# Scores, exponentials and value products reordered by two query tiles, and the 16-bit product rows copied on GpSimd from the second batch on

## The chip, the cores and the metric

One NeuronCore of a Trainium2 chip. The metric is the device time of the whole program in microseconds (us). In this document PE is TensorE (matmuls), PEld its weight loads, DVE is VectorE, ACT is ScalarE, POOL is GpSimd and SP is SyncE, whose queue issues the DMAs.

## What is computed

Two recurrent layers over an input of 4 batches, 512 tokens and 512 features. Each layer is a normalisation, an attention branch, a feed-forward branch, and `x = x + attention * silu(feed-forward)`. The change touches the first layer only, whose reference is, cut to what matters:

```python
xn = layernorm(x)
q = (xn @ Wq)   # 32 heads of 16
k = (xn @ Wk)   # 8 key heads of 16, each used by 4 query heads
v = (xn @ Wv)   # 8 value heads of 16
attn = softmax(einsum('bhqd,bhkd->bhqk', q, k) / 4).astype(float16)
s = einsum('bhqk,bhkd->bhqd', attn, v) @ Wo
y = fwht(xn * SU_ug) / 64
y = silu(y @ W_gate.T * scale_g) * (y @ W_up.T * scale_u)     # 2048 wide
g = silu((fwht(y * SU_dp) / 64) @ W_down.T * scale_d)
x = x + s * g
```

The second layer (a delta-rule recurrence and a sign feed-forward) follows and is the same in both kernels.

## The kernel before, in words

`layer0` writes one program for each engine, and all of them run over the same counter `t` of **steps**. The attention is cut into 32 **units** (4 batches x 8 key heads, `NKV`). A unit has 4 **query tiles** of 128 queries, and a query tile takes two steps, so a unit has `STEPS` = 8 steps, a batch `BSTEPS` = 64, and there are 256 steps with scores. `m` is the step within its batch. What happens to one query tile, for its group of 4 query heads:

- PE, even `t`: `scores(t // 2)` (L1106) makes 4 matmuls, one for each head, into 4 PSUM banks (`vpair` and `bank`). It waits until all 4 exponentials of the tile before are made, since there are only these 4 banks.
- DVE: `row_max` (L623), 4 reductions of 128x512, each for one bank.
- ACT: `exps` (L922), 4 exponentials of 128x512 into `probs` (3 buffers, `TAKEN`); two of them at step `t` and two at `t + 1`.
- SP, two steps later: `turn_probs` (L339) issues a DMA transpose of the whole tile from `probs` to its columns of `probsT`.
- PE, at `t % 8 == PV_STEP` = 2 of the unit after: `weigh(u)` (L1117) makes the 16 value products of the unit from all 4 turned tiles at once. It waits for the DMA transposes of all of them. It stands right behind the scores of that step.
- DVE: `to_tokens`, `divide`, `to_features` (L659 to L689) at steps 3, 4 and 6 of the next unit; POOL takes over the division (L450) from unit 5.

Beside the attention, PE works at the feed-forward branch, whose results go through two PSUM banks, `GB`. In steps `m >= FFN_STEP` = 32 of a batch (the **gate half**) each step is one chunk of 8 matmuls (`ffn_mm`, L1143): at even steps the gate of 128 rows, at odd steps the up projection. ACT makes the tanh of the gate (`tanh_gate`, L941) and DVE multiplies it (`gate_mul`, L633), which frees the gate's bank; DVE then forms the product rows in 32 bit (`up_mul`, L646, into `row32`, a part of `th`), which frees the up bank; ACT copies them to 16 bit (`high_rows`, L898) and POOL subtracts to get the low half (`low_rows`, L443). `up_mul` of the next rows waits for that subtraction, because `row32` is one buffer. In steps `m < 32` of the batch after (the **down half**) each step is 6 matmuls with these rows (`down_mm`, L1157 to L1159) and, four times, an output projection (`project_o`, L1102) and the residual. During the first batch the weights are prepared as well: steps 0 to 31 transform the up and gate weights (`transform_ug`, L1055, `high_half`, `low_half`, and `chunk_pairs` on POOL), steps 16 to 68 the down weights (`dn_pair` on POOL, L412, `transform_dn`, `high_down`, `low_down`).

The order on each engine is the order of the program text in the loop over `t`, written out by hand. Waits are semaphores, and a waiting instruction holds up all behind it on its engine. At an even step of the gate half PE has

```python
if t < NU * STEPS and t % 2 == 0:
    scores(t // 2)
if t % STEPS == PV_STEP and 0 <= t // STEPS - 1 < NU:
    weigh(t // STEPS - 1)
```

and behind it the 8 matmuls of the step. The keys and queries of a unit reach their 4 slots by `load_heads` (L300): 8 small DMAs in a row, issued by SP at `t % 8 == 6`, between the DMA transposes.

Of the kernel before, what the change touches and what calls it, by code (L numbers as in the profile page):

```python
# [11 lines left out]
P = 128  # L12
# [22 lines left out]
PV_STEP, TOKEN_STEP, DIVIDE_STEP, TURN_BACK = 2, 3, 4, 6  # L35
# [120 lines left out]
def layer0(nc, d, x1_dram, W):  # L156

    ctx = ExitStack()
    with ctx:  # L159
# [113 lines left out]
        def _(sp):  # L273
# [26 lines left out]
            def load_heads(u):  # L300
# [28 lines left out]
            def load_raw(i):  # L329
                if i == 0:  # L330
                    sp.wait_ge(S["pv_done"], NU)
# [7 lines left out]
            def turn_probs(n):  # L339
# [7 lines left out]
            load_heads(0)  # L347
            load_heads(1)
            sp.dma_start(wsd[:, :], d["wscale_dp"].partition_broadcast(P)).then_inc(S["wo_in"], 16)
            for t in range(TEND):  # L350
# [14 lines left out]
                if t % STEPS == STEPS - 2 and 1 < t // STEPS + 2 < NU:  # L365
                    load_heads(t // STEPS + 2)
# [15 lines left out]
        def _(pool):  # L382
# [55 lines left out]

            def low_rows(b, ft):
# [24 lines left out]
            for t in range(TEND):  # L464
# [28 lines left out]
                if fb < B and fm >= FFN_STEP and t % 2 == 0 and (fb or (fm - FFN_STEP) // 2 >= LOW_FIRST):  # L493
                    low_rows(fb, (fm - FFN_STEP) // 2)
# [6 lines left out]
        def _(v):  # L501
# [158 lines left out]
            def to_tokens(u):  # L660

                v.wait_ge(S["pv_done"], u + 1)
# [116 lines left out]
            for t in range(TEND):  # L779
# [35 lines left out]
                if t % STEPS == TURN_BACK and 0 <= t // STEPS - 1 < NU and t // STEPS % 2 == 0:  # L815
                    to_features(t // STEPS - 1)
# [22 lines left out]
        def _(a):  # L839
# [74 lines left out]
            def evict_v(b):  # L914

                a.wait_ge(S["mb_full"], MB["v", b] + 1)
                if b >= 2:
                    a.wait_ge(S["pv_done"], (b - 1) * NKV)
# [58 lines left out]
            for t in range(TEND):  # L977
# [12 lines left out]
                if 0 <= t - PREP - 2 < NCH * KT:  # L990
                    high_half(t - PREP - 2)
# [5 lines left out]
                if t % 16 == Q_STEP + 1 and t // 16 + 1 < NU // 2:  # L997
                    evict_q(t // 16 + 1)
                if m == V_STEP + 1 and b + 1 < B:
                    evict_v(b + 1)  # L1000
                if m == K_STEP + 1 and b + 1 < B:
                    evict_k(b + 1)
                if t > FFN_STEP + 1 and (t - 2) // BSTEPS < B and (t - 2) % BSTEPS >= FFN_STEP and t % 2 == 0:
# [1597 lines left out]
```

## Time and profile before

| | us |
|---|---|
| three timed runs, median (lowest to highest) | 1487.92 (1484.96 to 1489.20) |
| the profiled execution | 1479.72 |
| its span, first to last instruction | 1477.9 |
| busy in the span: PE, DVE, ACT, POOL | 1278.4, 1058.7, 775.1, 524.5 |
| first layer with scores, 21.4 to 782.5 | 761.1 |
| rest of the first layer, to about 850 | 67 |
| second layer, from about 850 | 628 |

The mean granted TensorE clock is 0.963 of full speed over the span. The times of this table are one execution and three others; the profiled one is 8.2 us below the median. In the stretch with scores PE, DVE and ACT work in lockstep on one query tile at a time, so the busy shares there say little by themselves: the start of each tile's scores is the beat, and what delays it is what costs.

### The profile page before, as it was taken

What the parts mean: (1) busy time and instruction counts of PE and PEld (TensorE: products, weight loads), DVE (VectorE), ACT (ScalarE), POOL (GpSimd) and SP (SyncE); (2) the same over time, 40 slices, a digit from 0 to 9 for tenths busy, and PEclk for the clock granted to TensorE, in tenths of its full rate; (3) what the DMA queues carried; (4) which work ended last, traced back from release to release, by engine and by line L of the source; (5) the groups of instructions that cost most, each with busy time, mean ns of one, the idle gap of its engine ahead of it and who ended that gap; (6) DMA issues with size and microseconds to landing.
All of it is one profiled execution on the core that took longest, in us unless ns stands there. A gap on an engine that the chain in (4) does not pass through costs nothing. (4 is left out here: it accounts for less than half of the span.)

```text
span 1477.9 us, 22423 instructions
## 1 busy us (share of the span) xinstructions
PE 1278.4 (87%) x8226; PEld 640.0 (43%) x8226; DVE 1058.7 (72%) x1823; ACT 775.1 (52%) x1308; POOL 524.5 (35%) x434
## 2 busy tenths in 40 slices
PE   4777788777877787877888899999999999999998
PEld 2232333232322233322333355585548654765466
DVE  6688877666766567656777498687878688669846
ACT  5676666554655557545661775236533554246532
POOL 2389853002210022100221156323733274317531
PEclk9899999998999999999999999999999999999999
DMA  7775545565555665565657502300230111210221
GB/s 242 187 168 99 92 91 90 105 123 104 92 104 98 130 114 98 106 119 114 112 102 227 212 20 55 86 16 29 55 71 23 37 45 43 55 37 19 55 48 44
DMA packets 346557, 135.52 MB, mean 92 GB/s; under 512 B 312176, under 2 KB 333392, under 8 KB 343888
## 3 DMA queue, kind: packets, MB, share of 16 engines
q1 hardware_dynamic: 334032, 132.52, 40.6%
q10 hardware_dynamic: 12416, 1.57, 1.0%
q8 instruction: 66, 1.08, 0.3%
q14 instruction: 43, 0.35, 0.1%
HBM read 44.87 MB, written 17.87 MB: 42 GB/s over the span
## 5 line engine op out<-in xcount | busy, mean ns | idle before, releaser
L929 ACT ACTIVATE probs<-vpair,top_n 128x512 f16<-128x512 f32 x256 | 164.4, 687 | 256.3 <-DVE top_n L627 256.3
L1143 PE MATMUL bank<-rows,both 128*128 128x512 f16 x1024 | 244.7, 392 | 5.2 <-DVE fd L700 4.1
L627 DVE TENSOR_REDUCE top_n<-vpair 128x1 f32<-128x512 f32 x256 | 164.5, 684 | 84.9 <-PE bank L1114 82.8
L443 POOL TENSOR_TENSOR h<-th,h 128x512 f16<-128x512 f32 x61 | 71.5, 1172 | 271.5 <-ACT h L898 271.5
L627 DVE TENSOR_REDUCE top_n<-bank 128x1 f32<-128x512 f32 x256 | 163.7, 681 | 0.0
L929 ACT ACTIVATE probs<-bank,top_n 128x512 f16<-128x512 f32 x256 | 162.6, 690 | 0.0
L1143 PEld LDWEIGHTS bank<-rows,both 128*128 128x128 f16 x1024 | 97.5, 100 | 144.5 <-issue 35.4
L2218 PE MATMUL bank<-rows,both 128*128 128x512 f16 x512 | 118.3, 382 | 0.0
L1114 PE MATMUL vpair<-qk 32*128 32x512 f16 x256 | 50.4, 389 | 74.4 <-ACT probs L929 74.4
L2234 PE MATMUL bank<-both,hid 128*128 128x512 f16 x512 | 111.2, 379 | 0.0
L1128 PE MATMUL bank<-probsT,vaug 128*32 128x512 f16 x512 | 45.3, 487 | 72.3 <-DMA probsT<-probs 60.4
L1157 PE MATMUL bank<-dn,h 128*128 128x512 f16 x256 | 104.1, 407 | 0.9 <-DVE tg L633 0.9
L2202 PE MATMUL bank<-rows,both 128*128 128x512 f16 (+1 forms) x456 | 104.0, 379 | 0.9 <-PEq L159 0.9
L1158 PE MATMUL bank<-dn,h 128*128 128x512 f16 x256 | 103.1, 403 | 0.0
L1159 PE MATMUL bank<-dn,h 128*128 128x512 f16 x256 | 102.4, 400 | 0.0
L633 DVE SCALAR_TENSOR_TENSOR tg<-tg,bank 128x512 f32<-128x512 f32 x64 | 44.0, 687 | 72.3 <-ACT tg L941 71.8
L456 POOL TENSOR_TENSOR otok<-oblk,rl 128x256 f16<-128x256 f32 x25 | 15.5, 620 | 180.0 <-DVE rl L673 180.0
L2234 PEld LDWEIGHTS bank<-both,hid 128*128 128x128 f16 x512 | 50.1, 98 | 60.4
L2218 PEld LDWEIGHTS bank<-rows,both 128*128 128x128 f16 x512 | 48.4, 100 | 55.4 <-issue 0.8
L1114 PEld LDWEIGHTS vpair<-qk 32*128 32x128 f16 x256 | 12.9, 91 | 131.3 <-ACT probs L929 74.2
L2202 PEld LDWEIGHTS bank<-rows,both 128*128 128x128 f16 (+1 forms) x456 | 43.6, 98 | 55.5 <-issue 4.4
L1593 POOL TENSOR_TENSOR big<-big,both 128x384 f32<-128x384 f32 x32 | 32.0, 1026 | 94.5 <-DMA big<-t_scratch 70.3
(362 smaller groups left out, 2673.3 us busy)
## 6 DMA issues: line engine op xcount, KB each, us to landing
h<-in_ug SPq DMA_DIRECT2D x8, 1024.0 KB, 5.8
lt_scratch<-big SPq DMA_DIRECT2D x16, 384.0 KB, 2.7
dn<-in_down SPq DMA_DIRECT2D x2, 2048.0 KB, 11.1
x_scratch<-th SPq DMA_DIRECT2D x16, 256.0 KB, 2.6
res<-x_scratch SPq DMA_DIRECT2D x16, 256.0 KB, 4.1
out_x<-res SPq DMA_DIRECT2D x16, 256.0 KB, 2.0
both<-in_w SPq DMA_DIRECT2D x2, 1548.0 KB, 11.9
t_scratch<-tok SPq DMA_DIRECT2D x16, 192.0 KB, 2.1
```

The source lines that it names most:

```text
L443: pool.tensor_tensor(h16(ft, 1), row32, h16(ft, 0), ALU.subtract).then_inc(S["row_lo"], 1)
L627: v.tensor_reduce(top_n[:, i:i + 1], SC_[n % G][:, :], AX.X, ALU.max, negate=True).then_inc(S["max_done"], 1)
L929: a.activation(probs[:, k % TAKEN, j * T:(j + 1) * T], SC_[j][:, :], ACT.Exp, bias=top_n[:, i:i + 1]).then_inc(S["p_ready"], 1)
L1114: pe.matmul(SC_[j][:, :], qs[32 * j:32 * j + 32, u % SLOTS, qt * P:(qt + 1) * P], ks[32 * j:32 * j + 32, u % SLOTS, :], start=True, stop=T ...
L1128: mm = pe.matmul(OB[32 * j:32 * j + 32, :], vaug[:, b % 2, kt, g, :], probsT[:, TT * j + kt, :], start=kt == 0, stop=kt == TT - 1)
L1143: mm = pe.matmul(GB[n % 2][:, :], w[:, kt, col:col + P], xnb(b, kt), start=r == 0, stop=r == 2 * KT - 1)
L1157: pe.matmul(bk, h16(ft, 0)[:, rows], dn16(ft, 0), start=j == 0, stop=False)
L1158: pe.matmul(bk, h16(ft, 0)[:, rows], dn16(ft, 1), start=False, stop=False)
L1159: mm = pe.matmul(bk, h16(ft, 1)[:, rows], dn16(ft, 0), start=False, stop=j == FT - 1)
L2202: mm = pe.matmul(bk, lhs(i, kt), rhs(j, kt), start=n == 0, stop=n == 3 * KT - 1)
L2218: mm = pe.matmul(fbank[ht % 2][:, :], up[:, kt, ht * P:(ht + 1) * P], x_half(i, kt), start=kt == 0 and i == 0, stop=kt == KT - 1 and i == 1)
L2234: mm = pe.matmul(fbank[tt % 2][:, :], hid[:, i, ht, tt * P:(tt + 1) * P], down[:, ht, :], start=ht == 0 and i == 0, stop=ht == HT - 1 and ...
```

## The change

1. The unit's value products are cut in two: `weigh(n)` now takes 2 query tiles (256 columns) and is called at `t % 4 == 0` for the pair whose scores began 8 and 6 steps earlier. Before, the last tile's scores began 4 steps earlier. `to_tokens`, `divide` and `to_features` move by 1, 2 and 4 steps.
2. `load_heads` is split: `load_k` at `t % 8 == 6`, `load_q` at `t % 8 == 2`.
3. Of the feed-forward matmuls of an even step, 4 or 3 (gate half, `GATE_AHEAD`) or 1 or 0 (down half, `DOWN_AHEAD`) now stand ahead of the scores; so do the turns of x and the weight transforms of the first batch.
4. On ACT, `high_half` (first batch) stands ahead of the exponentials; `high_rows` of the first batch moves to the front of the step; from the second batch on it is an instruction of POOL. Evictions of q, k and v come one step later from step 70 on, behind the second pair of exponentials.

```diff
-PV_STEP, TOKEN_STEP, DIVIDE_STEP, TURN_BACK = 2, 3, 4, 6
+TOKEN_STEP, DIVIDE_STEP, TURN_BACK = 4, 6, 2
+GATE_AHEAD, DOWN_AHEAD = (4, 3), (1, 0)
+LATE_EVICT = 70
...
-            def load_heads(u):
+            def load_k(u):
...
                 for j in range(G):
                     sp.dma_start(ks[32 * j:32 * j + DH, slot, :], kst[DH * g:DH * g + DH, :]).then_inc(S[f"heads_in{slot}"], 16)
+
+            def load_q(u):
+
+                slot = u % SLOTS
                 sp.wait_ge(S["mb_took"], MB["q", u // 2] + 1)
+                if u >= SLOTS:
+                    sp.wait_ge(S["s_ps"], (u - SLOTS + 1) * SC)
                 for j in range(G):
...
                 if u:
-                    sp.wait_ge(S["pv_done"], u)
+                    sp.wait_ge(S["pv_done"], n // 2 - 1)
                 sp.dma_start_transpose(probsT[:, :, qt * P:(qt + 1) * P], probs[:, n % TAKEN, :]).then_inc(S[f"pt_in{n % TAKEN}"], 16)
...
-                if t % STEPS == STEPS - 2 and 1 < t // STEPS + 2 < NU:
-                    load_heads(t // STEPS + 2)
+                if t % STEPS == 6 and t // STEPS + 2 < NU:
+                    load_k(t // STEPS + 2)
+                if t % STEPS == 2 and 1 < t // STEPS + 1 < NU:
+                    load_q(t // STEPS + 1)
...
+            def high_rows(b, ft):
+                pool.wait_ge(S["gb_took"], GO["gu", b, 2 * ft + 1] + 1)
+                pool.tensor_copy(h16(ft, 0), row32).then_inc(S["row_hi"], 1)
...
                 if fb < B and fm >= FFN_STEP and t % 2 == 0 and (fb or (fm - FFN_STEP) // 2 >= LOW_FIRST):
+                    if fb:
+                        high_rows(fb, (fm - FFN_STEP) // 2)
                     low_rows(fb, (fm - FFN_STEP) // 2)
...
+                if FFN_STEP + 1 < t < BSTEPS + 2 and t % 2 == 0:
+                    high_rows(0, ((t - 2) % BSTEPS - FFN_STEP) // 2)
                 if b < B and m > FFN_STEP and m % 2:
                     tanh_gate(b, (m - FFN_STEP) // 2)
+                if 0 <= t - PREP - 2 < NCH * KT:
+                    high_half(t - PREP - 2)
                 if t < NU * STEPS:
                     exps(2 * t)
                     exps(2 * t + 1)
                 if t in TURN_STEP:
                     evict_x(KT + TURN_STEP.index(t))
-                if 0 <= t - PREP - 2 < NCH * KT:
-                    high_half(t - PREP - 2)
...
-                if t % 16 == Q_STEP + 1 and t // 16 + 1 < NU // 2:
+                late = 1 if t < LATE_EVICT else 2
+                if t % 16 == Q_STEP + late and t // 16 + 1 < NU // 2:
                     evict_q(t // 16 + 1)
...
-                if t > FFN_STEP + 1 and (t - 2) // BSTEPS < B and (t - 2) % BSTEPS >= FFN_STEP and t % 2 == 0:
-                    high_rows((t - 2) // BSTEPS, ((t - 2) % BSTEPS - FFN_STEP) // 2)
...
-            def weigh(u):
-
+            def weigh(n):
+
+                u, half = divmod(n, 2)
                 b, g = divmod(u, NKV)
-                for i in range(TAKEN):
-                    pe.wait_ge(S[f"pt_in{i}"], 16 * ((TT * (u + 1) - 1 - i) // TAKEN + 1))
-                if u:
+                for k in (2 * n, 2 * n + 1):
+                    pe.wait_ge(S[f"pt_in{k % TAKEN}"], 16 * (k // TAKEN + 1))
+                if u and half == 0:
                     pe.wait_ge(S["o_free"], u)
...
+                cols = slice(2 * P * half, 2 * P * (half + 1))
                 for kt in range(TT):
                     for j in range(G):
-                        mm = pe.matmul(OB[32 * j:32 * j + 32, :], vaug[:, b % 2, kt, g, :], probsT[:, TT * j + kt, :],
+                        mm = pe.matmul(OB[32 * j:32 * j + 32, cols], vaug[:, b % 2, kt, g, :], probsT[:, TT * j + kt, cols],
                                        start=kt == 0, stop=kt == TT - 1)
...
-                if t < NU * STEPS and t % 2 == 0:
-                    scores(t // 2)
-                if t % STEPS == PV_STEP and 0 <= t // STEPS - 1 < NU:
-                    weigh(t // STEPS - 1)
...
+                ahead = 0
+                if t % 2 == 0:
+                    ahead = (DOWN_AHEAD if m < FFN_STEP else GATE_AHEAD)[t // 2 % 2]
+                ffn(t, 0, ahead)
+                if t < NU * STEPS and t % 2 == 0:
+                    scores(t // 2)
+                if t % 4 == 0 and 0 <= t // 4 - 2 < 2 * NU:
+                    weigh(t // 4 - 2)
+                ffn(t, ahead, 2 * KT)
```

PE, one unit in the gate half of the second batch, **before**: the whole unit's value products (`probsT,vaug`) once, ahead of the tile's 16 feed-forward matmuls (`rows,both`; `qk` are the scores, `rows,wq` a projection of queries).

```order
L1128 MATMUL bank<-probsT,vaug 32x512 x16
L1143 MATMUL bank<-rows,both 128x512 x16
L1114 MATMUL vpair<-qk 128x512 x2
L1114 MATMUL bank<-qk 128x512 x2
L1143 MATMUL bank<-rows,both 128x512 x16
L1074 MATMUL bank<-rows,wq 128x512 x4
L1114 MATMUL vpair<-qk 128x512 x2
L1114 MATMUL bank<-qk 128x512 x2
L1143 MATMUL bank<-rows,both 128x512 x16
L1114 MATMUL vpair<-qk 128x512 x2
L1114 MATMUL bank<-qk 128x512 x2
L1143 MATMUL bank<-rows,both 128x512 x16
```

PE, the same gate half **after**, from two steps earlier on (a projection of keys, `rows,wk`, falls into it): half the columns every second tile, and 3 or 4 of the 16 feed-forward matmuls now run before the scores that they followed.

```order
L1148 MATMUL bank<-probsT,vaug 32x256 x16
L1163 MATMUL bank<-rows,both 128x512 x15
L1132 MATMUL vpair<-qk 128x512 x2
L1132 MATMUL bank<-qk 128x512 x2
L1163 MATMUL bank<-rows,both 128x512 x17
L1132 MATMUL vpair<-qk 128x512 x2
L1132 MATMUL bank<-qk 128x512 x2
L1148 MATMUL bank<-probsT,vaug 32x256 x16
L1163 MATMUL bank<-rows,both 128x512 x12
L1100 MATMUL bank<-rows,wk 128x512 x4
L1163 MATMUL bank<-rows,both 128x512 x3
```

Between the value products and the next ones there are now two scores instead of four, and each product is half as wide; of every 16 feed-forward matmuls 3 or 4 have changed sides with the scores.

ACT, gate half, **before**: between the first pair of exponentials (`vpair`) and the second (`bank`) stand the copy of the product rows (`h<-th`) and the tanh (`tg<-bank`).

```order
L929 ACTIVATE probs<-vpair,top_n 128x512 x2
L898 ACTIVATE h<-th 128x512
L941 ACTIVATE tg<-bank,usc 128x512
L929 ACTIVATE probs<-bank,top_n 128x512 x2
L929 ACTIVATE probs<-vpair,top_n 128x512 x2
```

ACT, gate half of a later batch, **after**: only the tanh stands between them, and the values' eviction (`vaug<-bank`) follows the second pair.

```order
L946 ACTIVATE probs<-vpair,top_n 128x512 x2
L958 ACTIVATE tg<-bank,usc 128x512
L946 ACTIVATE probs<-bank,top_n 128x512 x2
L936 ACTIVATE vaug<-bank 128x32x16
L946 ACTIVATE probs<-vpair,top_n 128x512 x2
```

SP, one unit, **before**: 8 loads of keys and queries in a row, then the four transposes.

```order
L309 DMA qk<-kst 16x512 x4
L313 DMA qk<-qst 16x512 x4
L377 DMA x_scratch<-th 128x512
L345 DMA_TRANSPOSE probsT<-probs 128x16x128 x4
L309 DMA qk<-kst 16x512 x4
```

SP, one unit, **after**: at most 4 loads between two pairs of transposes.

```order
L311 DMA qk<-kst 16x512 x4
L388 DMA x_scratch<-th 128x512
L353 DMA_TRANSPOSE probsT<-probs 128x16x128 x2
L321 DMA qk<-qst 16x512 x4
L353 DMA_TRANSPOSE probsT<-probs 128x16x128 x2
L311 DMA qk<-kst 16x512 x4
```

## Rows read from the trace of the kernel before

**Rows 1.** Windows, half batches: us; busy PE, PEld, DVE, ACT, POOL; clock; DMA share.
```profile
21.40:138.90 117.50, 85.60 (x311) 34.39 (x311) 89.64 (x156) 86.82 (x150) 76.31 (x49) 0.93 0.70 168
138.90:242.90 104.00, 84.62 (x436) 32.98 (x437) 81.58 (x129) 65.48 (x112) 71.62 (x64) 0.98 0.48 87
242.90:327.90 85.00, 67.67 (x349) 25.33 (x348) 53.42 (x88) 45.20 (x74) 7.00 (x8) 0.92 0.62 117
327.90:427.20 99.30, 79.49 (x419) 31.13 (x420) 68.03 (x109) 58.96 (x100) 21.09 (x20) 0.91 0.54 96
427.20:513.50 86.30, 64.10 (x340) 23.84 (x341) 50.20 (x84) 42.86 (x70) 7.01 (x8) 0.90 0.59 116
513.50:605.50 92.00, 73.21 (x420) 29.80 (x420) 67.94 (x109) 58.95 (x100) 21.09 (x20) 0.98 0.59 104
605.50:690.20 84.70, 63.78 (x340) 23.84 (x341) 50.19 (x84) 42.86 (x70) 7.01 (x8) 0.92 0.63 118
690.20:782.50 92.30, 73.80 (x393) 28.64 (x394) 68.59 (x110) 57.24 (x97) 20.52 (x19) 0.94 0.56 102
```

**Rows 2.** Timeline, PE, a down half: start us, us, what, count, [idle before <- releaser].
```profile
267.19 0.39 PE L1114 MATMUL vpair<-qk 32*128 32x512 f16 x2 [0.58 <-ACT probs L929]
...
270.63 1.05 PE L1128 MATMUL bank<-probsT,vaug 128*32 128x512 f16 x16 [3.04 <-issue]
...
274.33 0.63 PE L1158 MATMUL bank<-dn,h 128*128 128x512 f16 x1
...
275.99 0.39 PE L1114 MATMUL vpair<-qk 32*128 32x512 f16 x2
...
279.68 0.39 PE L1114 MATMUL vpair<-qk 32*128 32x512 f16 x2 [0.59 <-ACT probs L929]
```

**Rows 3.** Timeline, SP, the same stretch.
```profile
263.56 2.48 SPq L313 DMA_DIRECT2D qk<-qst  x4
266.14 8.41 SPq L345 DMA_TRANSPOSE probsT<-probs  x2
```

**Rows 4.** The tile probsT in 242.9 to 782.5: the transposes and their landing.
```profile
L345 SPq DMA_TRANSPOSE probsT<-probs x96: 1317/1931/3318, 242.0 to 777.5; - x96
DMA to landing us min/median/max: 4.3/4.3/6.1
```

**Rows 5.** Timeline, a gate half: one tile on PE, DVE, ACT and POOL.
```profile
404.21 0.39 PE L1114 MATMUL vpair<-qk 32*128 32x512 f16 x2 [1.36 <-ACT probs L929]
404.54 3.63 PE L1143 MATMUL bank<-rows,both 128*128 128x512 f16 x16
405.35 1.28 ACT L929 ACTIVATE probs<-vpair,top_n 128x512 f16<-128x512 f32 x2 [1.28 <-DVE top_n L627]
406.53 0.62 ACT L898 ACTIVATE h<-th 128x512 f16<-128x512 f32 x1
407.05 0.68 ACT L941 ACTIVATE tg<-bank,usc 128x512 f32<-128x512 f32 x1
407.62 1.26 ACT L929 ACTIVATE probs<-bank,top_n 128x512 f16<-128x512 f32 x2
407.76 0.69 DVE L633 SCALAR_TENSOR_TENSOR tg<-tg,bank 128x512 f32<-128x512 f32 x1 [0.65 <-ACT tg L941]
```

**Rows 6.** Timeline, PE, the next two scores of the same gate half.
```profile
408.94 0.39 PE L1114 MATMUL vpair<-qk 32*128 32x512 f16 x2 [0.77 <-ACT probs L929]
...
417.37 0.39 PE L1114 MATMUL vpair<-qk 32*128 32x512 f16 x2 [0.21 <-ACT probs L929]
```

**Rows 7.** Groups by line, POOL: count, busy us, mean ns, idle before.
```profile
L443 POOL TENSOR_TENSOR h<-th,h 128x512 f16<-128x512 f32 x61 | 71.5, 1172 | 271.5 <-ACT h L898 271.5
...
L1518 POOL MEMSET big<- 128x768 f32 x1 | 0.7, 737 | 0.0
```

**Rows 8.** Windows, first batch, columns as in rows 1.
```profile
100.00:166.00 66.00, 48.56 (x212) 18.70 (x210) 56.18 (x99) 41.30 (x73) 64.54 (x53) 0.97 0.56 109
```

**Rows 9.** Waits between 60 and 100 us: us in total, times, longest.
```profile
PE bank L1128 <- DMA probsT<-probs: 5.1, 1, 5.1
```

More of the change, by code:

```diff
@@ L343, in turn_probs @@
                 if u:
-                    sp.wait_ge(S["pv_done"], u)
+                    sp.wait_ge(S["pv_done"], n // 2 - 1)
                 sp.dma_start_transpose(probsT[:, :, qt * P:(qt + 1) * P], probs[:, n % TAKEN, :]).then_inc(S[f"pt_in{n % TAKEN}"], 16)
-            load_heads(0)
-            load_heads(1)
+            for u in range(2):
+                load_k(u)
+                load_q(u)
             sp.dma_start(wsd[:, :], d["wscale_dp"].partition_broadcast(P)).then_inc(S["wo_in"], 16)
@@ L814, in _ @@
                     divide(t // STEPS - 1)
-                if t % STEPS == TURN_BACK and 0 <= t // STEPS - 1 < NU and t // STEPS % 2 == 0:
-                    to_features(t // STEPS - 1)
+                if t % STEPS == TURN_BACK and 0 <= t // STEPS - 2 < NU and t // STEPS % 2:
+                    to_features(t // STEPS - 2)
                 if b == B and m == 3:
@@ L996, in _ @@
                     high_down(DN_AT.index(t))
-                if t % 16 == Q_STEP + 1 and t // 16 + 1 < NU // 2:
+                late = 1 if t < LATE_EVICT else 2
+                if t % 16 == Q_STEP + late and t // 16 + 1 < NU // 2:
                     evict_q(t // 16 + 1)
-                if m == V_STEP + 1 and b + 1 < B:
+                if m == V_STEP + late and b + 1 < B:
                     evict_v(b + 1)
-                if m == K_STEP + 1 and b + 1 < B:
+                if m == K_STEP + late and b + 1 < B:
                     evict_k(b + 1)
-                if t > FFN_STEP + 1 and (t - 2) // BSTEPS < B and (t - 2) % BSTEPS >= FFN_STEP and t % 2 == 0:
-                    high_rows((t - 2) // BSTEPS, ((t - 2) % BSTEPS - FFN_STEP) // 2)
                 if b and m - 1 in DOWN_END:
@@ L1145, in ffn_mm, with down_mm, ffn @@
                     mm.then_inc(S["gb_full"], 1)
-            def down_mm(n, j):
+            def down_mm(n, j, r):
                 k, ft = GO["down", n], DN_TURN[j]
-                if j == 0:
+                if j == 0 and r == 0:
                     pe.wait_ge(S["gb_took"], k - 1)
-                if n % TT == 0:
+                if n % TT == 0 and r == 0:
                     pe.wait_ge(S["row_lo"], n // TT * FT + ft + 1)
-                if n == 0:
+                if n == 0 and r == 0:
                     pe.wait_ge(S["mb_took"], MB["dn", j] + 1)
                 bk, rows = GB[k % 2][:, :], slice(n % TT * P, (n % TT + 1) * P)
-                pe.matmul(bk, h16(ft, 0)[:, rows], dn16(ft, 0), start=j == 0, stop=False)
-                pe.matmul(bk, h16(ft, 0)[:, rows], dn16(ft, 1), start=False, stop=False)
-                mm = pe.matmul(bk, h16(ft, 1)[:, rows], dn16(ft, 0), start=False, stop=j == FT - 1)
-                if j == FT - 1:
+                mm = pe.matmul(bk, h16(ft, r // 2)[:, rows], dn16(ft, r % 2), start=j == 0 and r == 0, stop=j == FT - 1 and r == 2)
+                if j == FT - 1 and r == 2:
                     mm.then_inc(S["gb_full"], 1)
+            def ffn(t, first, last):
+                b, m = t // BSTEPS, t % BSTEPS
+                if b and m < FFN_STEP:
+                    for i in range(first, min(last, 6)):
+                        down_mm((b - 1) * TT + m // 8, 2 * (m % 8) + i // 3, i % 3)
+                if b < B and m >= FFN_STEP:
+                    for r in range(first, last):
+                        ffn_mm(b, m - FFN_STEP, r)
             def turn_next():
@@ L1208, in _ @@
                     transform_dn(DN_AT.index(t))
-                for half in range(2):
-                    if b and m < FFN_STEP:
-                        down_mm((b - 1) * TT + m // 8, 2 * (m % 8) + half)
-                    if b < B and m >= FFN_STEP:
-                        for r in range(KT * half, KT * half + KT):
-                            ffn_mm(b, m - FFN_STEP, r)
                 if t % 16 == Q_STEP and t // 16 + 1 < NU // 2:
```

8 lines of the change are left out of this document (4 added, 4 removed).

## The prediction

> **What bounds the kernel now.** I cut the span into half batches first [rows 1]: 2 of the first batch (117.5 and 104.0 us), then three down halves (85.0, 86.3, 84.7: 256.0 in all) and three gate halves (99.3, 92.0, 92.3: 283.6 in all). In none of the later six is an engine full: in 242.9 to 327.9 PE is busy for 67.67 of 85 us, DVE for 53.42, ACT for 45.20. Something makes them all wait. Behind 782.5 comes the rest, about 695 us, whose work and order the change leaves alone.
>
> The timeline shows it. In a down half one tile's scores follow another's after 279.68 - 275.99 = 3.69 us, which is the loop of scores, four reductions and four exponentials on 4 banks. But from 267.19 to 275.99 are 8.80 us [rows 2]: PE sits before the value products from about 267.6 to 270.63, and the next scores stand behind them and behind the 12 feed-forward matmuls. This happens in every unit, at the second tile. What PE waits for is the last tile's DMA transpose. It was issued at 266.14 [rows 3] and lands 4.3 us later [rows 4], at about 270.4. Part of that is SP's own queue: the loads of keys and queries ran until 266.04 [rows 3], while the tile's exponentials were all made when the scores before those of 267.19 could start, one beat earlier, at about 263.5: 2.6 us lost. And after the wait PE runs slowly: one shows 0.63 us at 274.33 where the scores, of as many columns, show 0.39 [rows 2]; the mean granted clock of such halves is 0.90 to 0.92 [rows 1].
>
> In a gate half the beat is 408.94 - 404.21 = 4.73 us without the wait and 417.37 - 408.94 = 8.43 with it [rows 5, 6]. Rows 5 give the chain of the 4.73: scores at 404.21, first exponentials at 405.35 (1.14 later), two exponentials 1.28, the copy of the product rows until 407.15, the tanh from 407.05 until 407.73, two exponentials until 408.88, next scores 408.94. PE's 16 feed-forward matmuls are started by 404.54 + 3.63 - 0.39 = 407.78, one each 0.216 us (15 such steps and one of 0.39), so PE has a second to spare.
>
> **The change, part by part.** *Value products later and in halves, loads split.* A pair's last scores now lie 3 tiles before its products. At 3.7 us a tile, its exponentials are finished 3.7 us after its scores, the transpose can wait behind 1.93 us of the transpose before and 2.5 us of four loads [rows 3, 4], of which 3.7 pass meanwhile, so it is issued about 0.8 us late and lands 4.3 us later: 8.8 us after its scores. The products are reached at 11.1. I take the wait as gone, with 2 us to spare. Its price per unit is the long interval less the short one: 8.80 - 3.69 = 5.1 in the down half, 8.43 - 4.73 = 3.7 in the gate half. Over 12 units each: 61 and 44 us. What takes its place: the products of 512 columns keep PE for about 1.05 us [rows 2]; two of 256 columns have the same columns in all but 32 weight loads for 16. No row has the narrow ones. They cost between nothing more and another 1.05 us a unit; the 16 weight loads beside the nearest row point to some 0.1 to 0.2. With the division and turns of the heads on other tiles I give 4 us of the down halves back: **-57**. Gate halves from this: **-44**.
>
> SP must not become the bound. Per unit it issues 4 transposes of 1.93 us and 8 loads of 0.63 (2.48 / 4, rounded up for the gaps) [rows 3, 4]: 12.8 us, and in the down half one input tile and one result more, some 14. Four tiles of the down half will take 16.3. That is nearly full, and it is where the forecast can slip.
>
> *Gate half: the rows' copy off ACT, matmuls ahead.* Without the copy (0.62 us) ACT's chain closes at 4.73 - 0.62 = 4.1 us, or at 1.14 + 1.28 + 0.68 + 1.26 = 4.36 if its instructions don't overlap. Another loop gets longer. DVE's gate product (L633) needs the tanh, and DVE has finished its reductions 0.65 us before it; its own 0.69 us then end about 3.8 us after the scores instead of 4.24 (407.76 + 0.69 - 404.21) [rows 5]. Only then is the gate's bank free for the 3 or 4 matmuls that now stand before the scores: 3 or 4 x 0.216 + 0.1 = 0.75 to 0.96. So tiles take 4.55 to 4.8 us; I take 4.6. Sum: 48 tiles x (4.73 - 4.6) = **-6**. The evictions placed one step later (0.6 us each, 20 of them) leave ACT's chain; some of that is in the 8.43 already and I count nothing.
>
> *The copy on POOL.* It adds 48 instructions of 128x512 to POOL, which is busy 21 of 92 to 99 us there [rows 1]. No row shows a POOL copy. The nearest are the subtraction of the same rows, 1.17 us with two inputs, from above, and a fill of 768 columns, 0.74 us, that is 0.49 for 512, from below [rows 7]. I take 0.8, near their middle. The product rows' buffer then turns round in 0.7 (as L633 [rows 5]) + 0.8 + 1.17 and some 0.3 of handing over = 3.0 us (3.4 at the upper end), under the beat of 4.6. Hidden by that, it costs nothing; if the cover went, each us above a period of 4.6 would cost 48 us. The Trainium skill (GPSIMD Engine Reference, section 4.1) speaks against such a move: elementwise work with two inputs is about twice as slow on GpSimd as on VectorE, with one input roughly line-rate. This case's trace has the subtraction at 1.17 us beside 0.69 of a VectorE operation of that size [rows 5, 7], and by that rule the copy would be nearer my lower end; the sum stays as it is.
>
> *First batch.* The only long wait of PE for a transpose is one of 5.1 us [rows 9]; it goes. Taking one 0.62 to 0.69 us operation out of ACT's chain (`high_half` or `high_rows`) could save 0.6 on each of 32 tiles, 20 us. But from 100 to 166 us POOL is busy 64.54 of 66 [rows 8], with butterflies of the weights that both parts wait for; there I count nothing. That leaves about 21 tiles x 0.6 = 13. Bounds: 5 if only the wait goes, 30 if PE's transforms ahead of the scores help as well. **-18**.
>
> **The sum:** 57 + 44 + 6 + 18 = 125 us. The profiled execution takes 1479.7 us, so 1354.7; the median of the timed runs lies 8.2 above it, and I forecast it: 1487.9 - 125 = **1363 us**. A measurement of this kernel can tell about 0.3% (4.5 us) from no change.
>
> **Clock.** In the stretch with the matmuls of 0.63 us the granted clock is below full, the others are at the upper of its two levels, 2.4 GHz; before the slow ones PE had waited 3.04 us [rows 2]. The Trainium skill (TensorE: Matmul & The Clock Gate, part 1) says that idle gaps put PE back to half its clock. By that rule the halves should show a mean clock of nearly 1.0. The price is inside the long intervals that I took whole, so it is not added.
>
> **The rivals.**
> (a) *The wait comes back by SP.* For: 14 of 16.3 us are taken; the transposes' issue varies from 1.3 to 3.3 us [rows 4]; two waits per unit now instead of one. Against: DMA share 0.62 [rows 1], and 2 us to spare. If each transpose costs SP 2.6 to 3.3 us instead of 1.93, a unit of the down half takes 16.8 to 19.5 us, up to 3.2 more than 16.3, which is up to 38 us over 12 units: 1363 to 1401, the middle 1385. Chance 0.17.
> (b) *The gate loop is longer than its sum.* The matmuls ahead wait for DVE, which is busy 68.03 / 16 = 4.25 us a tile [rows 1]. At 5.0 us a tile the gate halves lose 48 x 0.4 = 19 us: 1382. Chance 0.12.
> (c) *More than counted.* If PE alone sets the gate's beat (16 x 0.216 + 0.33 for scores + 0.5 of products = 4.3) and the first batch gives 30: 1363 - 14 - 12 = 1337. Chance 0.10.
> (d) *Slower.* The copy on POOL closes a loop: DVE's product rows, the copy, the subtraction, the next product rows. With a copy of c us its period is 2.2 + c. It decides from c = 2.4 on. Before, gate tiles took 283.6 / 48 = 5.9 us; to eat also the 75 us of the other parts the period must be 5.9 + 75 / 48 = 7.5, so c = 5.3; at 6 it would give 1488 - 75 + 48 x 2.3 = 1523. Against it: both POOL rows end below 1.2 us. Chance 0.03.
> (e) *The change doesn't do what it says:* the transposes are late for the pairs as well, since each beat that gets shorter also brings the products nearer. Then PE waits as long as now, and only the 6 + 13 remain: 1469. Chance 0.03.
> My forecast, 1345 to 1380, has 0.55.
>
> **The numbers.** 1363; range 1335 to 1402, which takes in (a), (b) and most of (c). Faster: all but (d) and a small part of (e): 0.96; same 0.01; slower 0.03.
>
> **What would show it.** After: no interval between scores of 8 us or more from the second batch on; PE's wait for the transposes under 10 us there in all, in place of 3 us a unit; down halves near 66 us, gate halves near 78, clock at least 0.97; the POOL copy between 0.5 and 1.2 us; 782.5 becomes about 657. Wrong would be: PE waiting before the products in most units (a or e), gate tiles at 5 us with PE idle ahead of the feed-forward matmuls until DVE's gate product (b), DVE waiting for POOL's rows (d), or a first batch that is as long as before.

## The result, and the profile after

The changed kernel takes 1392.1 us (median of 4 runs, 1387.96 to 1394.73) against 1486.66 us for the kernel before on the same chip: a ratio of 0.936, 95% interval 0.9331 to 0.9389. Forecast were 1363 us with a range of 1335 to 1402. The range holds it; of the 125 us that the sum promised, 94.6 came. Its profiled execution takes 1387.96 us against 1479.72 for that of the kernel before, a difference of 91.8 us, and all comparisons by stretch below are between such executions. The changed kernel's lies 4 us below its median, so differences by stretch can add up to a few us less than those of medians.

Windows of the kernel after, from the first scores of one half batch to those of the next (the last ends a little behind the last scores). Columns as in [rows 1].

```profile
25.10:155.50 130.40, 88.46 (x359) 33.42 (x358) 91.72 (x158) 85.64 (x144) 86.32 (x62) 0.90 0.65 153
155.50:252.80 97.30, 84.61 (x498) 33.38 (x497) 76.76 (x121) 66.55 (x111) 61.29 (x51) 0.98 0.50 90
252.80:322.50 69.70, 62.62 (x420) 25.31 (x419) 53.62 (x89) 46.00 (x75) 6.08 (x8) 1.00 0.75 137
322.50:403.60 81.10, 72.90 (x479) 29.16 (x479) 67.83 (x109) 50.86 (x85) 31.08 (x36) 1.00 0.71 123
403.60:467.70 64.10, 58.78 (x409) 23.96 (x411) 49.80 (x84) 42.46 (x69) 6.67 (x9) 1.00 0.83 147
467.70:547.90 80.20, 72.80 (x478) 29.23 (x478) 67.80 (x109) 50.96 (x85) 31.09 (x36) 1.00 0.71 126
547.90:612.20 64.30, 58.84 (x407) 23.99 (x408) 49.83 (x84) 42.40 (x69) 6.85 (x9) 1.00 0.78 146
612.20:691.00 78.80, 70.22 (x452) 27.12 (x452) 66.69 (x108) 48.38 (x81) 30.28 (x35) 1.00 0.72 127
```

Beside [rows 1]: the down halves fell from 85.0, 86.3 and 84.7 us to 69.7, 64.1 and 64.3, and the clock went from 0.90 to 0.92 up to 1.00. The first two gate halves fell from 99.3 and 92.0 to 81.1 and 80.2. But the first half batch **rose** from 117.5 to 130.4 us, and it begins at 25.1 instead of 21.4. Of the 33 us that the profiled executions fall short of 125, 28 are in the first batch with its later beginning, and 8.5 in the gate halves.

| stretch, profiled executions | before | after | change | forecast |
|---|---|---|---|---|
| to the first scores | 21.4 | 25.1 | +3.7 | 0 |
| first half batch | 117.5 | 130.4 | +12.9 | -18 for both |
| second half batch | 104.0 | 97.3 | -6.7 | |
| three down halves | 256.0 | 198.1 | -57.9 | -57 |
| three gate halves (the last to its last scores: 87.3 and 75.6) | 278.4 | 236.9 | -41.5 | -50 |
| all behind the last scores | 702.2 | 700.1 | -2.1 | 0 |

The scores now follow each other in a down half without the long interval of [rows 2], and the products stand between them without a wait. Timeline, PE, down half of the kernel after:

```profile
273.74 0.39 PE L1132 MATMUL vpair<-qk 32*128 32x512 f16 x2 [0.47 <-ACT probs L946]
...
274.07 0.62 PE L1148 MATMUL bank<-probsT,vaug 128*32 128x256 f16 x16
277.41 0.39 PE L1132 MATMUL vpair<-qk 32*128 32x512 f16 x2 [0.24 <-ACT probs L946]
...
281.09 0.39 PE L1132 MATMUL vpair<-qk 32*128 32x512 f16 x2 [0.38 <-ACT probs L946]
```

The transposes behave as forecast. The tile `probsT` of the kernel after, 252.8 to 691, beside [rows 4]: each issue takes a little longer, and none is waited for to speak of. Behind it, from the page, POOL's copy and subtraction.

```profile
L353 SPq DMA_TRANSPOSE probsT<-probs x96: 1742/2022/3481, 252.5 to 687.1; - x96
...
DMA to landing us min/median/max: 4.2/4.5/6.6
```
```profile
L458 POOL TENSOR_TENSOR h<-th,h 128x512 f16<-128x512 f32 x61 | 70.5, 1155 | 39.1 <-ACT h L915 35.2
L452 POOL CAST h<-th 128x512 f16<-128x512 f32 x48 | 29.2, 609 | 123.9 <-DVE th L663 123.9
```

What is new is in the first half batch. Timelines, kernel after, first PE and then ACT:

```profile
63.23 0.38 PE L1052 MATMUL bank<-ident,both 128*128 128x128 f16 x4 [2.51 <-ACT rows L878]
63.45 1.52 PE L1073 MATMUL bank<-h,had 128*128 128x512 f32 x2
64.76 1.91 PE L1074 MATMUL bank<-h,nhad 128*128 128x512 f32 x2
66.60 0.60 PE L1132 MATMUL vpair<-qk 32*128 32x512 f16 x2
```
```profile
61.34 1.26 ACT L946 ACTIVATE probs<-bank,top_n 128x512 f16<-128x512 f32 x2
62.48 0.60 ACT L878 ACTIVATE rows<-bank 128x512 f16<-128x512 f16 x1
...
66.71 0.69 ACT L896 ACTIVATE both<-bank,suc 128x512 f16<-128x512 f32 x1 [2.59 <-PE bank L1074]
67.97 1.28 ACT L946 ACTIVATE probs<-vpair,top_n 128x512 f16<-128x512 f32 x2 [0.58 <-DVE top_n L644]
```

ACT finishes a tile's exponentials at 62.6 and only then evicts the turned x (L878), that is, copies it out of its PSUM bank, which PE's next turn (L1052) needs. PE waits 2.51 us for it, then transforms, and starts the scores at 66.6, 4 us after the exponentials that they had waited for before. ACT in its turn waits 2.59 us for that transform (`high_half`, L896), because it now stands ahead of the exponentials. Each engine has the other's work in front of its own: a loop through both that was not there before.

In the gate half PE waits for DVE's gate product (L650) at the matmuls that were moved ahead of the scores. Timeline, kernel after:

```profile
388.47 0.75 DVE L663 SCALAR_TENSOR_TENSOR th<-bank,hsc,tg 128x512 f32<-128x512 f32 x1
388.49 0.33 PEld L1163 LDWEIGHTS bank<-rows,both 128*128 128x128 f16 x3 [0.64 <-DVE tg L650]
389.24 0.09 PEld L1132 LDWEIGHTS vpair<-qk 32*128 32x128 f16 x2 [0.42 <-ACT probs L946]
...
392.07 0.70 DVE L706 STREAM_TRANSPOSE oT<-otok 128x512 f16<-128x512 f16 x1
...
392.69 0.65 DVE L650 SCALAR_TENSOR_TENSOR tg<-tg,bank 128x512 f32<-128x512 f32 x1
...
393.40 1.04 PE L1163 MATMUL bank<-rows,both 128*128 128x512 f16 x4 [0.85 <-DVE tg L650]
...
394.37 0.39 PE L1132 MATMUL vpair<-qk 32*128 32x512 f16 x2
```

The exponentials of the tile were made at 388.87 and 393.42 (L946: 387.61 and 392.15, 1.26 and 1.27 us long); the scores came at 389.25 and 394.37, 0.4 and 0.95 us later.

### The profile page after: what moved, and what is told of

The parts are those of the page before. It is cut to its first block and busy times, and to the rows that moved or that the text cites. A ratio compares the mean times of both kernels' runs of the same rounds, so it can differ in the third digit from the quotient of the medians.

```text
span 1386.1 us, 23478 instructions
## 1 busy us (share of the span) xinstructions
PE 1258.4 (91%) x8738; PEld 636.7 (46%) x8738; DVE 1055.1 (76%) x1823; ACT 753.6 (54%) x1260; POOL 553.8 (40%) x482
## 5 line engine op out<-in xcount | busy, mean ns | idle before, releaser
L946 ACT ACTIVATE probs<-vpair,top_n 128x512 f16<-128x512 f32 x256 | 164.3, 687 | 167.0 <-DVE top_n L644 163.5
L1177 PE MATMUL bank<-dn,h 128*128 128x512 f16 x768 | 179.1, 382 | 4.0 <-DVE fd L717 2.1
L1163 PEld LDWEIGHTS bank<-rows,both 128*128 128x128 f16 x1024 | 91.1, 98 | 165.1 <-DVE tg L650 43.5
L946 ACT ACTIVATE probs<-bank,top_n 128x512 f16<-128x512 f32 x256 | 162.8, 690 | 0.0
L1177 PEld LDWEIGHTS bank<-dn,h 128*128 128x128 f16 x768 | 71.4, 98 | 97.1 <-issue 14.5
L2229 PE MATMUL bank<-rows,both 128*128 128x512 f16 (+1 forms) x456 | 104.0, 379 | 0.9 <-PEq L161 0.9
L452 POOL CAST h<-th 128x512 f16<-128x512 f32 x48 | 29.2, 609 | 123.9 <-DVE th L663 123.9
L2245 PEld LDWEIGHTS bank<-rows,both 128*128 128x128 f16 x512 | 48.4, 100 | 55.4 <-issue 1.0
L1132 PE MATMUL vpair<-qk 32*128 32x512 f16 x256 | 50.8, 392 | 13.2 <-ACT probs L946 12.9
L1574 POOL TENSOR_TENSOR hid<-sil 128x512 f32<-128x512 f32 x24 | 33.1, 1378 | 62.5 <-DVE sil L1694 62.5
L663 DVE SCALAR_TENSOR_TENSOR th<-bank,hsc,tg 128x512 f32<-128x512 f32 x64 | 48.0, 750 | 10.6 <-DMA x_scratch<-th 7.5
L1634 POOL TENSOR_TENSOR os_<-os_,both 128x6 f32<-128x6 f32 x16 | 23.3, 1458 | 80.6 <-DVE os_ L1992 80.6
## 6 DMA issues: line engine op xcount, KB each, us to landing
x_scratch<-th SPq DMA_DIRECT2D x16, 256.0 KB, 3.0
res<-x_scratch SPq DMA_DIRECT2D x16, 256.0 KB, 4.1
out_x<-res SPq DMA_DIRECT2D x16, 256.0 KB, 2.0
```

The costliest lines, as they stand in the source:

```text
L663: v.scalar_tensor_tensor(row32, GB[n % 2][:, :], hsc[:, ft:ft + 1], tg[:, :], ALU.mult, ALU.mult).then_inc(S["gb_took"], 1)
L946: a.activation(probs[:, k % TAKEN, j * T:(j + 1) * T], SC_[j][:, :], ACT.Exp, bias=top_n[:, i:i + 1]).then_inc(S["p_ready"], 1)
L1132: pe.matmul(SC_[j][:, :], qs[32 * j:32 * j + 32, u % SLOTS, qt * P:(qt + 1) * P], ks[32 * j:32 * j + 32, u % SLOTS, :], start=True, stop=T ...
L1163: mm = pe.matmul(GB[n % 2][:, :], w[:, kt, col:col + P], xnb(b, kt), start=r == 0, stop=r == 2 * KT - 1)
L1177: mm = pe.matmul(bk, h16(ft, r // 2)[:, rows], dn16(ft, r % 2), start=j == 0 and r == 0, stop=j == FT - 1 and r == 2)
L1574: pool.tensor_tensor(sqf[m % 2], sil[:, ORDER[m], :], sil[:, ORDER[m], :], ALU.mult).then_inc(S["sq_r"], 1)
```

## The experiments

Twelve kernels, each timed beside the kernel before. Medians are of 4 executions (e12: of 5), and are given with their ratio to the kernel before and its 95% interval. e1 to e4, e8 and e9 start from the changed kernel and put one or two parts back; e5 joins e2 and e3, and e10 to e12 start from e5; e6 and e7 start from the kernel before.

**e1: PE's turns and transforms behind the scores again.**

```diff
                 if t % 4 == 0 and 0 <= t // 4 - 2 < 2 * NU:
                     weigh(t // 4 - 2)
+                if t in TURN_STEP:
+                    turn_x(KT + TURN_STEP.index(t))
+                if 0 <= t - PREP - 2 < NCH * KT:
+                    transform_ug(t - PREP - 2)
```

> Changed kernel, but PE's turns of x and weight transforms (steps 0 to 31) stand behind the scores and value products again; ACT's high_half stays ahead of the exponentials. Theory A (in the first half batch the scores wait for a turn that waits for ACT's eviction, and then for 1.7 to 3.4 us of transforms): the first half batch falls from 130.5 us to about 115 to 120, the intervals of 12.9 and 13.1 us shrink below 10, total about 1378 (1372 to 1384). Rival B (the first half batch is set by the weights' preparation on POOL, ACT and DVE, wherever PE's work stands): first half 128 to 132, total 1389 to 1394.

Measured: 1391.3 us, ratio 0.9381 (0.9341 to 0.9421), the same as the changed kernel. The first half batch is 138.7 us, worse than 130.4, though it begins at 22.1 again: the later beginning comes from the turns and transforms ahead of PE's first scores. Theory A as I had put it, that the place on PE is what costs, falls. B is not right either, as e2 shows. Waits of e1 in 22 to 160 us, in total, times, longest; then the same of the changed kernel in 25 to 155:

```profile
ACT both L896 <- PE bank L1074: 48.8, 17, 4.5
...
PE vpair L1132 <- ACT probs L946: 28.0, 13, 4.3
```
```profile
ACT both L896 <- PE bank L1074: 32.1, 19, 3.0
...
PE bank L1052 <- ACT rows L878: 19.6, 7, 4.2
```

With the transform back behind the scores, ACT's `high_half` ahead of the exponentials waits even longer, and the scores wait for the exponentials behind it. The loop is the same, entered at another place.

**e2: as e1, and ACT's high_half behind the exponentials and evictions again.**

```diff
-                if 0 <= t - PREP - 2 < NCH * KT:
-                    high_half(t - PREP - 2)
                 if t < NU * STEPS:
...
                 if t in TURN_STEP:
                     evict_x(KT + TURN_STEP.index(t))
+                if 0 <= t - PREP - 2 < NCH * KT:
+                    high_half(t - PREP - 2)
```

> As e1_pe_back, and ACT's high_half stands behind the exponentials and evictions again. Theory A: with PE's transform behind the scores, a high_half ahead of the exponentials waits for it, so putting it back gains again: first half 110 to 115, total about 1372 (1366 to 1378). Rival C (taking high_half out of ACT's chain is a gain of its own): 3 to 10 us slower than e1_pe_back.

Measured: 1376.3 us, ratio 0.9281 (0.9239 to 0.9322); 15 us faster than e1, and 16 than the changed kernel. First half batch 118.7 us (its window, columns as above), as before the change:

```profile
21.80:140.50 118.70, 89.31 (x363) 36.32 (x363) 93.84 (x162) 87.18 (x150) 80.31 (x55) 0.90 0.71 170
```

ACT's wait for the transforms is no longer among the longest. The total is in theory A's range, the first half batch is 3.7 us above it. Rival C falls.

**e9: only ACT's high_half back,** PE's order as in the changed kernel (the second hunk of e2 alone).

> Changed kernel with only ACT's high_half back behind the exponentials and evictions; PE's turns and transforms stay ahead of the scores. Theory M (ACT's half is the cause: high_half ahead of the exponentials waits for a transform that waits, through the turn, for ACT's own last eviction): first half batch 116 to 121, total 1373 to 1379, as e2_both_back. Rival N (both must go back, since the transforms ahead also hold the scores for 1.7 us or more): first half 124 to 130, total 1381 to 1390.

Measured: 1383.7 us, ratio 0.9317 (0.9283 to 0.935); first half batch 122.9, and it starts at 25.5 us. N is right within its total, M is not: ACT's place gives about 8 us, PE's about another 7 once ACT's is back. The intervals of the ratios overlap on both sides, so the split is rough; the traces agree with it, since the first half batch ends at 155.5 us in the changed kernel, at 148.4 here and at 140.5 in e2. Alone, PE's gives nothing (e1).

**e3: no feed-forward matmuls ahead of the scores.**

```diff
-GATE_AHEAD, DOWN_AHEAD = (4, 3), (1, 0)
+GATE_AHEAD, DOWN_AHEAD = (0, 0), (0, 0)
```

> Changed kernel without feed-forward matmuls ahead of the scores (GATE_AHEAD and DOWN_AHEAD zero), nothing else. Theory D (in the gate half the matmuls ahead wait for DVE's gate product and hold the scores): PE's wait for it, 20 us, goes, tiles with few products get shorter and those with value products longer, because the tanh then comes later; gate halves 75 to 82 us instead of 80, total 1386 to 1396. Rival E (the 4 and 3 ahead are what makes the gate beat): gate tiles 5.1 or more, total 1402 to 1415.

Measured: 1373.9 us, ratio 0.9266 (0.9225 to 0.9306), **18 us faster** than the changed kernel, which is below the ranges of both theories; the direction and the tiles are D's. Its first two gate halves (windows) are 77.4 and 76.1 us in place of 81.1 and 80.2:

```profile
319.80:397.20 77.40, 72.04 (x484) 30.45 (x484) 67.12 (x109) 51.56 (x85) 31.17 (x36) 1.00 0.73 128
461.60:537.70 76.10, 71.84 (x480) 30.47 (x480) 67.02 (x109) 51.55 (x85) 31.18 (x36) 1.00 0.73 130
```

The timeline of two tiles, PE and ACT, beside that of the changed kernel above:

```profile
378.93 0.39 PE L1132 MATMUL vpair<-qk 32*128 32x512 f16 x2 [0.36 <-ACT probs L946]
...
381.75 0.69 ACT L958 ACTIVATE tg<-bank,usc 128x512 f32<-128x512 f32 x1 [0.40 <-PE bank L1163]
...
383.65 0.39 PE L1132 MATMUL vpair<-qk 32*128 32x512 f16 x2 [0.21 <-ACT probs L946]
...
388.00 0.39 PE L1132 MATMUL vpair<-qk 32*128 32x512 f16 x2 [0.40 <-ACT probs L946]
```

The tile with products takes 4.72 us and loses 0.40 of it in ACT's tanh, which waits for the gate's last matmul; that is what the matmuls ahead were good for (4.54 in the changed kernel). The tile without products takes 4.35 us, where the changed kernel has 5.12, because nothing there holds the scores back. By the starts of the scores the three gate halves take 224.4 us, 12.5 less than in the changed kernel, and another 3.2 come from the second half batch.

**e4: the 16-bit copy of the product rows on ACT in all batches,** at the front of the step.

```diff
-                    if fb:
-                        high_rows(fb, (fm - FFN_STEP) // 2)
                     low_rows(fb, (fm - FFN_STEP) // 2)
...
-                if FFN_STEP + 1 < t < BSTEPS + 2 and t % 2 == 0:
-                    high_rows(0, ((t - 2) % BSTEPS - FFN_STEP) // 2)
+                if t > FFN_STEP + 1 and (t - 2) // BSTEPS < B and (t - 2) % BSTEPS >= FFN_STEP and t % 2 == 0:
+                    high_rows((t - 2) // BSTEPS, ((t - 2) % BSTEPS - FFN_STEP) // 2)
```

> Changed kernel, but the 16-bit copy of the product rows stays on ACT in all batches, at the front of the step, ahead of the exponentials, where the changed kernel has it in the first batch. Theory F (the gate beat is set by DVE's gate product and the matmuls behind it, and ACT is idle at the front of the step): no change, 1389 to 1396. Rival G (the copy is worth its 0.62 us on each of 48 tiles): 1412 to 1422.

Measured: 1391.8 us, ratio 0.9386 (0.9338 to 0.9433): no change. ACT has 1.3 us without work at the front of such a tile, and the copy fits in. But here PE's matmuls ahead set the beat, so e10 asks again without them.

**e5: both losses taken out,** the edits of e2 and e3 together.

> Changed kernel with both losses taken out: no feed-forward matmuls ahead of the scores (as e3_none_ahead), and PE's turns and transforms and ACT's high_half behind (as e2_both_back). Theory A+D (two separate losses in different halves): the gains add, 1392 - 16 - 18 = 1358 (1354 to 1363); first half batch 118 to 119, gate halves 71 to 78. Rival H (a half batch that is entered earlier gives part back): 1364 to 1372.

Measured: 1358.4 us, ratio 0.9159 (0.9123 to 0.9195). The medians' gains add to the microsecond (1392 - 16 - 18 = 1358); H falls. The first half batch is 112.2 us, 6 less than expected. Half of that is its last interval, 8.17 us in e2 and 5.10 here, the first with gate matmuls ahead of the next scores. The gate halves, 76.9 us twice, are as expected. This version is 34 us faster than the changed kernel and 128 faster than the one before.

**e10: e5 with the copy on ACT,** as in e4.

> e5_none_both with the 16-bit copy of the rows on ACT in all batches, at the front of the step. Theory O (ACT waits 1.3 us for the reductions there, the copy of 0.62 us fits into it once the product rows are there): 1357 to 1364. Rival G (with nothing ahead ACT's chain is the beat again and each copy adds its 0.3 to 0.6 us on 48 tiles): 1372 to 1388.

Measured: 1359.5 us, ratio 0.9154 (0.9121 to 0.9187): no difference from e5. At the front of the step the copy costs nothing on either engine. Before, it stood between the two pairs of exponentials. No run moves it alone, but the last four intervals of e6's first gate half (below), where it still stands there, are 4.73, 4.86, 4.74 and 4.93 us, and those of e5 4.72, 4.35, 4.71 and 4.44. Loads in one row (e8) or early evictions (e11) leave these four as they are. So its place is what cost, up to 0.5 us a tile, and not the engine.

**e6: the kernel before with only the value products cut in two and taken later.** The edit is the change's `weigh`, its waits in `turn_probs` and the step numbers of `to_tokens`, `divide` and `to_features`; all else is as before.

> Kernel before with only the value products cut in two and taken later, and what follows on VectorE (steps 4, 6 and 2); loads of keys and queries together, nothing ahead of the scores, high_half and the rows' copy on ACT at their old places, evictions early. Theory I (the later products alone end the wait, since the transposes land 7 us after the tile's exponentials and the products come after 7.4 or more): PE waits under 15 us for transposes in all, down halves 64 to 68, gate halves 78 to 83, total 1372 to 1388. Rival J (the loads between the transposes still make them late): PE still waits 1 us or more a unit, total 1400 to 1430.

Measured: 1383.8 us, ratio 0.9326 (0.9291 to 0.9362). Theory I holds, though the first down half (71.4 us) is above its range of 64 to 68. This one part is worth 102 us, more than the whole change; the runs of e6 (1382 to 1385) and of the changed kernel (1388 to 1395) don't overlap. No run separates taking the products later from cutting them in two. PE's waits for transposes in 240 to 785 us, first in the kernel before, where 24.2 more stand at its weight loads, then in e6:

```profile
PE bank L1128 <- DMA probsT<-probs: 54.3, 19, 4.7
```
```profile
PE bank L1145 <- DMA probsT<-probs: 1.3, 3, 0.6
```

Its first down half and gate half of these batches are 71.4 and 83.1 us, at a clock of 1.00. By the starts of the scores all three gate halves take 242.0 us, against 278.4 before.

```profile
237.00:308.40 71.40, 62.08 (x412) 25.04 (x412) 53.73 (x89) 45.64 (x75) 5.89 (x8) 1.00 0.76 139
308.40:391.50 83.10, 72.15 (x484) 30.49 (x484) 68.22 (x109) 58.61 (x100) 22.29 (x22) 1.00 0.60 116
```

**e7: the kernel before with only the loads split.**

```diff
-                if t % STEPS == STEPS - 2 and 1 < t // STEPS + 2 < NU:
-                    load_heads(t // STEPS + 2)
+                if t % STEPS == 6 and t // STEPS + 2 < NU:
+                    load_k(t // STEPS + 2)
+                if t % STEPS == 2 and 1 < t // STEPS + 1 < NU:
+                    load_q(t // STEPS + 1)
```

> Kernel before with only the loads split (keys at step 6, queries at step 2 of a unit); products of the whole unit at their old place. Theory K (2.6 of the 3.0 us that PE waits are SP's queue): PE's wait a unit falls from 3 to about 1 us, the long intervals from 8.8 to 5.5 to 6.5, the clock recovers, total 1400 to 1425. Rival L (the loads are off the transposes' path): wait as before, 1478 to 1490.

Measured: 1435.9 us, ratio 0.9682 (0.9638 to 0.9726). The direction is K's; the size is not. Some units do better than K says (intervals of 4.6 and 4.7 us in place of 8.8 and 10.0 in units 9 and 11, which lie in the second batch), but others keep a long one, and in the gate halves of the second and third batch one grew to 10.6 us, from 8.7 and 7.1. PE is not waiting for a transpose there. Timeline, ACT, e7:

```profile
373.15 1.29 ACT L938 ACTIVATE probs<-vpair,top_n 128x512 f16<-128x512 f32 x2 [1.23 <-DVE top_n L636]
379.67 0.60 ACT L914 ACTIVATE kst<-bank 128x512 f16<-128x512 f32 x1 [5.24 <-DMA qk<-qst]
```

The eviction of the next batch's keys waits until all loads of this batch have landed, those of the last unit's queries too, and these now come 4 steps, half a unit, later than the keys. It stands between the two pairs of exponentials, so the tile waits with it. In the trace of the kernel before this eviction doesn't wait for a load.

**e11: e5 with the evictions of q, k and v one step earlier.**

```diff
-LATE_EVICT = 70
+LATE_EVICT = 999
```

> e5_none_both with the evictions of q, k and v one step earlier (LATE_EVICT out of reach). Theory P (each of the 18 or so stands inside ACT's chain again and costs its 0.6 us, and some of the values' and keys' more): 1366 to 1374. Rival Q (they are hidden): 1356 to 1361. It also tells what of the 8 us of e8_loads_together belongs to the evictions.

Measured: 1373.5 us, ratio 0.925 (0.9221 to 0.9279), 15 us slower than e5. P's number is right, and only a part of its reason. Most of the loss lies in the gate halves (84.8 and 82.4 us in place of 76.9 and 76.9: 13.4 of 15), in one unit of each, where the intervals are 7.96 and 8.23 us instead of 4.22 and 5.3 (7.94 and 6.94 in the third batch):

```profile
354.88 0.60 ACT L922 ACTIVATE kst<-bank 128x512 f16<-128x512 f32 x1 [3.14 <-DMA qk<-qst]
```

It is the wait of e7 again. The rest are evictions inside the chain at about 0.45 us each (4.22 in place of 3.77 us in units 8 and 10).

**e8: the changed kernel with the 8 loads in one row,** and early evictions.

```diff
                 if t % STEPS == 6 and t // STEPS + 2 < NU:
                     load_k(t // STEPS + 2)
-                if t % STEPS == 2 and 1 < t // STEPS + 1 < NU:
-                    load_q(t // STEPS + 1)
+                    load_q(t // STEPS + 2)
```

> Changed kernel with the 8 loads of a unit in one row again (step 6), and evictions one step earlier, as these loads need them. Theory I (the later products have enough room): 1389 to 1398, PE waits for transposes under 10 us more. Rival J: down halves 3 us longer each or more, total above 1402.

Measured: 1400.3 us, ratio 0.9445 (0.9407 to 0.9483), 8 us slower than the changed kernel and between the two numbers. Down halves of 70.7, 65.5 and 66.4 us show the small evictions, not 3 us of waiting, and PE's waits for transposes are 1.5 us in all. J falls, and I's total was too low by 2 us. So split loads and late evictions together are worth 8 us in the changed kernel. What of that belongs to the loads alone was not separated.

**e12: e5 with one gate matmul ahead in the tiles with products.**

```diff
-GATE_AHEAD, DOWN_AHEAD = (0, 0), (0, 0)
+GATE_AHEAD, DOWN_AHEAD = (1, 0), (0, 0)
```

> e5_none_both with 1 gate matmul ahead of the scores in the tiles with value products, none elsewhere. Theory D (any matmul ahead waits for DVE's gate product, which ends when the exponentials end): the tile that follows gains at most 0.2 us and the one before loses 0.1 to 0.3, total 1356 to 1363. Rival R (a small number ahead is the right dose): 1350 to 1354.

Measured: 1357.0 us, ratio 0.9132 (0.9106 to 0.9159). The tile with products goes from 4.72 to 4.50, the one before it in the other kind of unit from 4.35 to 4.61. The gate halves are 76.4 and 75.1 in place of 76.9 us, but the intervals of the ratios overlap for the most part, so the two can't be told apart by their times. D's range holds it, R's does not.

From these the whole can be put together. Later products: 1486 to 1384, -102 (e6). Split loads, late evictions and the copy out of the exponentials: 1384 to 1359, -24 (e10); with e8's 8 for the first two, some 16 of it are left for the copy, an estimate. Copy on POOL: nothing. Matmuls ahead: +18. Transforms and `high_half` ahead: +16. That is 1392 or 1393.

## Why the prediction was right or wrong, point by point

- *What bounds the kernel:* right. The long interval was the wait for the last transpose, and e6 alone takes it out.
- *Value products later, -57 and -44:* right in the mechanism and for the down halves, which gave 57.9 with the split loads. In the gate halves e6 gives 36 us for the products alone (278.4 to 242.0), 8 short of 44: the interval that had the wait now averages 5.4 us and not the 4.73 that I put in its place. That 4.73 was the shortest tile of its half batch, whose tiles without the wait average 4.99. The wait is gone, the room of 2 us was there, and the narrow products take 0.55 us (0.62 for the group, less its tail) twice a unit, so 0.1 more than the wide ones, as taken.
- *SP nearly full:* rival (a) did not come. Issues grew from 1.93 to 2.02 us, and the DMA share to 0.83, without a wait.
- *Gate half, tiles of 4.6 us, -6:* **the tile was mis-sized**, and that -6 nearly came is luck. I had the loop right (DVE's gate product, then the matmuls ahead, then the scores), and priced it from the tanh alone. That gives 4.55 us with 3 matmuls ahead and 4.76 with 4, and the trace has tiles of 4.54 and 4.76; but the other two of the pattern are 4.91 and 5.12, mean 4.83. There DVE also turns heads back or to tokens (0.7 us, L706 and L682), the gate product ends some 0.4 us later, and with it the scores. From e6 to the changed kernel the gate halves give 5 us (242.0 to 236.9); without matmuls ahead (e3) it would be 18, and the matmuls ahead take 12.5 of them back. Rival (b) named this wait and gave it 19 us; e3 shows 18 in the medians. I gave it a chance of 0.12 because I had set 4.6 as the beat, when ACT's chain without the copy was 4.36 by my own working. I never priced the change without its matmuls ahead.
- *The copy on POOL costs nothing:* right, 0.61 us where I took 0.8. The Trainium skill (GPSIMD Engine Reference, section 4.1) has elementwise work with one input at roughly line-rate there, and the trace agrees: the copy takes 609 ns, as ACT's 0.62 us, where the subtraction with two inputs takes 1155. That it also *gains* nothing there (e4, e10) I had not seen; ACT's front of the step was free.
- *First batch, -18:* **wrong in sign**: 12.9 - 6.7 + 3.7 = +10. **This step failed**: an operation taken out of ACT's chain was to save 0.6 us on each of 21 tiles. I counted what left the chain and not what the moved instruction waits for in its new place. `high_half` ahead of the exponentials waits for a transform, which waits through the turn for ACT's eviction behind the exponentials. Putting both back gives 16 us (e2), half of what was missing from the sum. And the saving itself never came: by the trace the scores of the second batch begin at 242.9 us before, at 237.0 in e6, which has no other order of ACT's or PE's work there, at 240.3 in e2 and at 232.8 in e5. So without the loop the first batch gives 3 to 10 us, not 18; what took its place as the bound there was not followed.
- *Evictions one step later: counted as nothing.* Wrong. They guard against a wait that the split loads make (e7, e11), and the two belong together; with split loads 15 us hang on them (e11), and the pair is worth 8 (e8).
- *Clock:* right, 1.00 in all six later half batches, where PE no longer stands still for 3 us in each unit. The trace agrees there with the Trainium skill's rule on idle gaps (TensorE: Matmul & The Clock Gate, part 1). In the first half batch it went from 0.93 to 0.90; e2 has 0.90 as well, so the new loop is not shown to be the cause.

## What to carry to other kernels

An instruction that is moved up an in-order queue takes its waits with it: before counting what leaves the chain, follow what it waits for back through the other engines, and see whether that path crosses the queue it now heads. Filling a wait with work from further back pays only if that work is ready when the wait begins; here 3 or 4 matmuls that needed the last result of the tile cost 18 us. And a change made of many reorderings is worth taking apart: one of its parts alone was faster than all of them together, and e5, 34 us faster than the whole change, lacks two.

## What the runs showed that I had not expected

Two losses, 16 us in the first half batch and 18 mostly in the gate halves, added without remainder in the medians: in this kernel a later half batch that starts earlier runs just as long (69.7 and 64.1 us for the first two down halves with and without the 16 us of e2). A DMA wait can also hide in an eviction: a wait of 3.14 us for a DMA's landing goes with two intervals of 7.96 and 8.23 us in e11, where e5 has 4.22 and 5.3 in the same unit: 6.7 us, twice the wait itself. What stands behind the eviction on ACT, exponentials and a tanh, is late with it; how the rest comes about I did not follow.
